# Reordering TensorE's and ScalarE's queues at the head of the merged loop of a transformer and recurrent layer pair

## The reference, cut to what matters

```
xa = ln(x);  sx = previous row of xa - xa                     # along the sequence
xxx = tanh((xa + sx * maa_x) @ maa_w1).reshape(b, l, 5, 32)   # the mixer
xxx = einsum('blfd,fde->blfe', xxx, maa_w2)
xk, xw, xv, xr, xg = xa + sx * (maa_stack + xxx)              # five mixed inputs
w = exp(-exp(time_decay + tanh(xw @ td_w1) @ td_w2))
r, k, v, g = xr @ Wr.T, xk @ Wk.T, xv @ Wv.T, silu(xg @ Wg.T)
per head, per step:  a = k v^T;  out = r (u * a + s);  s = a + w * s
og = groupnorm(out) ;  x1 = x + og * g @ Wo.T
xc = ln(x1);  mixed with its previous row;  x1 + sigmoid(xr2 @ Wfr.T) * (relu(xk2 @ Wfk.T)^2 @ Wfv.T)
```

## Time and profile before

| | before |
|---|---|
| median of 3 runs | 1112.36 us (1111.42 to 1115.19) |
| the profiled execution | 1112.93 us |
| its span, first to last instruction | 1111.1 us |
| TensorE busy | 1054.2 us, 95% |
| VectorE busy | 889.2 us, 80% |
| ScalarE busy | 767.4 us, 69% |
| GpSimd busy | 607.4 us, 55% |
| TensorE's granted clock, mean | 0.992 |

### The profile page before, as it was taken

How to read it: one execution, slowest core, us unless ns; L and a number is a source line. 1 busy time by engine, 2 the same in 40 slices (tenths; PEclk the granted TensorE clock), 3 DMA queues, 4 the chain that set the end, 5 groups by cost and what they waited for, 6 DMA issues and landing times.

```text
span 1111.1 us, 34641 instructions
## 1 busy us (share of the span) xinstructions
PE 1054.2 (95%) x12992; PEld 880.4 (79%) x12992; DVE 889.2 (80%) x1532; ACT 767.4 (69%) x1910; POOL 607.4 (55%) x535
## 2 busy tenths in 40 slices
PE   5899999999999998999999999999999999887888
PEld 4789899888899887777787787788787787666677
DVE  5987777888777776127999999999999999999643
ACT  4778778777777775566666766666776667744774
POOL 4777887877878875024433444443444443453332
PEclk9999999999999998999999999999999999999999
DMA  8500000011111110003333321333321233304011
GB/s 325 181 4 1 0 0 2 3 41 41 46 43 38 42 44 2 1 14 82 77 86 86 86 59 40 73 85 85 85 68 39 64 86 86 86 17 107 20 38 58
DMA packets 39868, 65.01 MB, mean 59 GB/s; under 512 B 4384, under 2 KB 26208, under 8 KB 39392
## 3 DMA queue, kind: packets, MB, share of 16 engines
q1 hardware_dynamic: 39776, 63.75, 21.5%
HBM read 55.35 MB, written 8.39 MB: 57 GB/s over the span
## 4 chain that ended last, share of the span: by engine, by line
PE 84%; DVE 8%; issue 4%; ACT 3%; POOL 1%; DMA 0%; ACTq 0%; DVEq 0%; POOLq 0%
PE psum L1010 10%; PE psum L1001 10%; PE psum L353 9%; PE psum L1091 9%; PE psum L267 6%; PE psum L336 5%; PE psum L368 5%; PE psum L297 4%; PE psum L280 3%; PE psum L1050 3%; PE psum L1130 2%; PE psum L1163 2%; PE psum L310 2%; PE psum L1272 2%; DVE shared L1832 2%
## 5 line engine op out<-in xcount | busy, mean ns | idle before, releaser
L1832 DVE TENSOR_TENSOR_SCAN shared<-late_wT,shared 128x512 f32<-128x512 f32 x128 | 194.0, 1516 | 0.0
L232 POOL TENSOR_TENSOR shared<-shared,att_row_max 128x512 f32<-128x512 f32 x128 | 132.4, 1054 | 16.9 <-DVE att_row_max L564 16.9
L453 ACT ACTIVATE shared<-shared 128x512 f32<-128x512 f32 x128 | 80.4, 631 | 69.7 <-POOL shared L232 69.6
L353 PE MATMUL psum<-shared 128*128 128x128 f32 x1024 | 126.0, 276 | 1.0 <-ACT shared L462 1.0
L1001 PE MATMUL psum<-late_glnT,w 128*128 128x256 f32 x512 | 119.8, 387 | 1.8 <-ACT late_glnT L1380 1.8
L353 PEld LDWEIGHTS psum<-shared 128*128 128x128 f32 x1024 | 120.2, 193 | 1.4 <-ACT shared L462 1.4
L1010 PE MATMUL psum<-w,late_hT 128*128 128x256 f32 x512 | 120.0, 383 | 1.3 <-ACT late_hT L1389 1.2
L564 DVE TENSOR_REDUCE att_row_max<-shared 128x8 f32<-128x512 f32 x128 | 86.9, 680 | 40.9 <-POOL shared L225 40.9
L896 POOL TENSOR_TENSOR late_xm<-late_mixed,late_xa 128x512 f32<-128x512 f32 x64 | 78.0, 1228 | 72.6 <-DVE late_mixed L1798 72.6
L1001 PEld LDWEIGHTS psum<-late_glnT,w 128*128 128x128 f32 x512 | 95.9, 192 | 18.0 <-issue 2.8
L905 POOL TENSOR_TENSOR shared<-shared,late_rT 128x512 f32<-128x512 f32 x32 | 40.7, 1270 | 122.9 <-DVE shared L1832 122.9
(11 more groups left out here) (169 smaller groups left out, 2474.6 us busy)
## 6 DMA issues: line engine op xcount, KB each, us to landing
shared<-v_rows SPq DMA_DIRECT2D x64, 512.0 KB, 7.6
shared<-in_enc SPq DMA_DIRECT2D x64, 128.0 KB, 2.6
v_rows<-shared SPq DMA_DIRECT2D x64, 64.0 KB, 1.8
out<-x SPq DMA_DIRECT2D x16, 256.0 KB, 2.0
x<-in_x SPq DMA_DIRECT2D x7, 512.0 KB, 9.8
w<-in_w SPq DMA_DIRECT2D x2, 1024.0 KB, 17.0
shared<-in_cross_mask SPq DMA_DIRECT2D x1, 1024.0 KB, 11.4
shared<-in_w_qkv SPq DMA_DIRECT2D x1, 768.0 KB, 4.7
```

What stands on the lines that cost most here:

```text
L232: nc.gpsimd.tensor_tensor(zs, zs, peak.unsqueeze(2).to_broadcast([P, PAIRS, S]), ALU.subtract).then_inc(shifted, 1)
L353: last = nc.tensor.matmul(dst[:, half * P:(half + 1) * P], w[:, kb, c0 + half * P:c0 + (half + 1) * P], src[:, u % 2, kb, 0:P], start=(kb ...
L453: nc.scalar.activation(probs[:, u % 2, half * 4:(half + 1) * 4, :].rearrange("p r k -> p (r k)"), z[:, u % 2, half, :], ACT.Exp).then_inc( ...
L1832: nc.vector.tensor_tensor_scan(states, wT[:, u, half, :, :, :].rearrange("p j b t -> p (j b t)"), states, 0.0, ALU.mult, ALU.add).then_inc ...
```

## The change

It moves three steps in TensorE's body and two in ScalarE's. TensorE: the MLP's transposes go from ahead of `transpose_on` to behind the gate's projection; `mixer(s + 1)` goes from behind `project_out` to ahead of the two `sum_heads`. ScalarE: the gate's tanh goes ahead of `mlp_copy_in`, and the mixer's tanh ahead of the two `set_states`. No instruction is added or taken away, and no wait changes.

```diff
@@ TensorE, body
                 if now:
                     project(s, NR)
-                if mlp_run:
-                    mlp_transpose(s + 3)
                 if there(s - 2):
                     transpose_on(s - 2)
                 if early(s - 1):
                     ch_values(early_run(s - 1, 1), 1)
                 if now:
                     project(s, NG)
+                if mlp_run:
+                    mlp_transpose(s + 3)
                 if early(s):
                     ch_transpose(early_run(s, 0), 0)
+                if mixing:
+                    mixer(s + 1)
                 if old:
                     sum_heads(s - 1, 2)
                     sum_heads(s - 1, 3)
...
                 if there(s - 2):
                     project_out(s - 2)
-                if mixing:
-                    mixer(s + 1)
@@ ScalarE, body
+                if there(s):
+                    copy(s, u, NG)
                 if there(s + 3):
                     mlp_copy_in(s + 3)
-                if there(s):
-                    copy(s, u, NG)
...
                 if early(s):
                     ch_copy_in(early_run(s, 0), 0)
+                if there(s + 1):
+                    mixer(s + 1)
                 if there(s - 1) and there(s):
                     set_states(s, 2)
                     set_states(s, 3)
-                if there(s + 1):
-                    mixer(s + 1)
```

## The result

| | before | after |
|---|---|---|
| median of 22 runs each, side by side | 1115.26 us | 1119.95 us |
| ratio, with its 95% interval | | 1.0046 (1.0033 to 1.0058) |
| mean granted TensorE clock of the 21 undisturbed runs | | 0.987 |
| the profiled execution | 1112.93 us | 1123.37 us |
| its span, granted clock | 1111.1 us, 0.992 | 1121.6 us, 0.981 |

What follows compares the result with a forecast made beforehand. TensorE's queue was taken as the bound through body 12, VectorE from body 13 on. +1.8 us through body 12 and +1.8 in bodies 13 and 14 made +3.6 on 1112.36: 1116.0 us, range 1110.2 to 1119.5.

Steps and rivals of the forecast that it cites:

- The hole ahead of the mixer: Ahead of `mixer`, TensorE waits for xin: 0.28 us in bodies 2 to 12, 0.72 in bodies 0 and 1.
- The cold start behind it: Behind the hole the first step, `mixer`'s four full matmuls, runs 0.10 us longer: 1.06 instead of 0.96.
- The excursion: Switching TensorE from full products to 32-column matmuls costs about 0.33 us; one saved a body, bodies 1 to 12.
- The period 33.3: The time of one loop body would be 33.3 us after the change.
- rival 3: No excursion saved, as narrow part to head sums costs as much: 4.0 us on top, 1120.0 us, chance 0.09.
- "beside": Narrow part of `mixer` hidden beside the head sums: taken as zero; if hidden, another -0.4 us a body.
- xin's 4.55 us behind the receptance: From the receptance's first matmul to xin's end stays 4.55 us, set by GpSimd's `make_bonus`.
- an xin that merely overlapped: If xin overlapped `make_bonus` and took 0.87 us, the hole would be 0.13 us, the total 1.7 us lower.
- The loop as a whole: Through body 12, +1.8 us on TensorE's path: body 0 +0.7, body 1 +0.5, bodies 2 to 12 +0.6.
- `add_bonus` waited: VectorE's idle time ahead of `add_bonus`: about 1.6 us in body 13, 0.5 in body 14; together +1.8 us.
- the sentence on bodies 13 and 14: There TensorE's idle time would shrink and nothing would wait for it; no cost was added for it.
- rivals 3 and 4: Besides rival 3, a second wait appears in the loop: 0.3 us a body, +3.3, 1119.3 us, chance 0.1.

Runs made afterwards that it cites:

- the filled change: The whole change plus four extra full products (1.73 us, no output) ahead of `mix_pair` in bodies 13 and 14, against the kernel before: ratio 1.0028.
- both filled kernels: The filled change, and the new order in bodies 13 and 14 alone with the same four products: ratios 1.0028 and 1.0026 to the kernel before.
- the shifted kernel: Order of before, `mixer` narrow part first between head sums and bonus sums in bodies 1 to 12, four extra products in body 12: ratio 0.9978 to kernel before.

## Why the prediction was right in its priced steps and short in its sum

**Right.** The hole ahead of the mixer: forecast 0.28 us in the loop, measured 0.27; forecast 0.72 in bodies 0 and 1, measured 0.72 and 0.71. The cold start behind it: 1.06 us for the four products, as forecast. The excursion: 0.33 us, confirmed alone by moving the bonus sums between. The period 33.3: 33.28, rival 3 (no saving) excluded by 33.61 in that experiment. That nothing is gained from "beside" beyond the excursion: the two narrow steps take 1.43 us, 0.56 + 1.00 less 0.13, the share of the excursion that falls on them (the rest is saved behind the gate and at `up`). xin's 4.55 us behind the receptance, and that GpSimd's `make_bonus` sets it. (The total for an xin that merely overlapped, 1.7 us lower, counted bodies 2 to 12 alone; body 0 would add 1.30 - 0.87 = 0.43.) The loop as a whole: the receptance of body 13 begins at 933.43 instead of 930.98, 2.45 us later, of which 0.79 were there when the merged loop began, ahead of anything that the change moves (the MLP's transposes of body -2, at 461.69 against 460.90; this execution had the extra half clock at 27 us), so 1.7 against the 1.8 forecast; the experiment on these bodies alone measured 1.0015. In body 13 `add_bonus` waited 1.58 us (forecast 1.6), in body 14 0.41 (forecast 0.5).

**Wrong.** The step that failed is the sentence on bodies 13 and 14: "TensorE's idle time there (the ScalarE tanh is now taken beside the head sums) shrinks, but nothing waits for it." Both halves of it fail, and the sum had this term at nothing. The idle time grew: body 13's stretch before has 36.94 - 31.22 = 5.7 us of it, the filled change at full clock 38.25 - 32.80 = 5.5 although 1.73 us of filling are in it, so 7.2 without. And more of it comes in one piece. Before, the mixer stood between the output projection and `mix_pair`, and idle times of 0.91 and 1.42 us followed it; after it is 2.05 us in both bodies, since `mix_pair` also waits for `add_residual` (L1895), which the later bonus sums had pushed back. And idle time on an engine that isn't the bound had a price here, through the clock: in the profiled execution 7.1 us of wait on VectorE; in the mean about 1.5 us, by which 1.0046 exceeds the forecast's 1.0033, while filling the idle time gave back 2.0 and 1.6. The times alone would not prove it, since 1.0033 is the lower end of the interval; the mean clock does more, 0.987 and 0.984 unfilled against 0.991 in both filled kernels. I had the ingredients: the trace of before has a stretch of half clock at 982 us, 1.5 us behind the end of its idle time of 1.42. I did not price it since the chain there ran through VectorE. No rival of mine named the clock.

The measured median of 1119.95 us lies 3.95 above my 1116.0. Of that, 2.9 are the kernel before, which itself ran above the median that I had started from, and 1.1 are the difference of the two medians, 4.7 instead of 3.6. The range took no account of how loosely three runs fix that median: here 20 of the 22 runs of before lie between 1111.4 and 1118 us. Nor did its upper end follow from its own terms: it says "up to rivals 3 and 4" but stops at 1119.5, below the 1120.0 that rival 3's sum gives. That the measured median falls on rival 3's 1120.0 is chance, for the excursion was saved.

## What to carry to other kernels

In a loop where TensorE is the bound, put steps that use few columns next to each other: each excursion from full products costs about 0.33 us here, and it costs nothing to avoid as long as the step doesn't have to start before its operand is there. Before a step is moved ahead, follow its operand back through the other queues; xin hung on GpSimd's product, two engines away from the mixer. And where TensorE is not the bound, its idle time is still not always free: here pieces of 1.4 to 2.2 us were followed by half clock in some executions. Look at the granted clock around each gap before moving work out of it.

## What the runs showed of the hardware that I had not expected

A kernel with work added came out faster: eight matmul records of 1.73 us in each of two bodies went with a ratio of 1.0028 instead of 1.0046 and a mean granted clock of 0.991 instead of 0.987. The Trainium skill ("TensorE: Matmul & The Clock Gate", section "Part 1: The HAM clock gate") says that the clock is released by activity and falls back when the array goes idle. The runs agree in part: in the profiled execution of the change it fell behind both idle times of 2.05 us. But the same idle time doesn't always bring it down. With the new order in bodies 13 and 14 alone, the 2.05 us in body 13 were followed by full clock. Some 2.2 us ahead of the keys of body 14 were followed by half clock in the kernel with the late bodies as before, and by full clock in the one with xin ahead of the scan. And 1.53 us were followed by half clock in the shifted kernel but not in the kernel before. So the same changed kernel took 1114.3 to 1116.0 us at a mean clock of 0.992 and 1123.1 to 1124.7 at 0.981. What decides it between executions no run here shows.
